# GpSimd's scatters in the scan stage, moved to other slots

## The chip, the cores and the metric

The kernel runs on one core of a Trainium2 chip. The metric is the device time of one execution in microseconds (us): from the program's start to its last output. TensorE (PE) multiplies matrices, VectorE (DVE) and GpSimd (POOL) do elementwise work, ScalarE (ACT) evaluates functions, SyncE (SP) issues most of the data transfers. Each engine runs its own list of instructions in order and waits for the others by semaphores.

## What is computed

The input is 8 sequences of 512 tokens with 256 features. Each goes through a Mamba layer, a residual and a layer norm, and then through a mixture of 8 experts of which each token takes 4, again with residual and norm:

```python
# per sequence, for t in 0..511, with h of 256 x 16:
dA = jnp.exp(dtt[:, :, None] * A)
h = h * dA + dtt[:, :, None] * Bt[:, None, :] * xt[:, :, None]
y = jnp.einsum('bdn,bn->bd', h, Ct) + xt * D
...
x = _layernorm(x + _L0_attn_ref(x, ...))
x = _layernorm(x + _L0_ffn_ref(x, ...))   # router, top 4 of 8 experts, SwiGLU
```

## The kernel before

There are two large stages. In the **scan stage** the 8 sequences run through a pipeline of rounds; in the **expert stage** tiles of 512 rows run through the experts' weights. Between them lies a queue in DRAM for each expert: a token's row (1088 bytes) is copied to the four queues of its experts. These copies are the **scatters** of line 1199: one is an indirect DMA that GpSimd issues, 128 rows long, and a sequence has 16, numbered 0 to 15.

A round has 16 **slots**, one for each of the 16 states of the scan. In round r (0 to 7; rounds 3 to 6 are the passes of a hardware loop of two rounds) the following is done at once:

- Sequence r is scanned. In slot t VectorE multiplies the input by B (`weigh_inputs`, line 1021, from PSUM and SBUF to PSUM) and runs the recurrence over 1024 columns (`scan`, line 1030), with the factors `decay` that ScalarE computes two slots ahead (`decays`, line 811). GpSimd multiplies the state by C (`read_state`, line 1157); in slot t it does this for state t-1. TensorE adds the products up (`sum_states`, line 630), in slot t for state t-2; the last two of a sequence come in slots 0 and 1 of the next round.
- Sequence r+1 is prepared: projection, convolution, SiLU, softplus. VectorE's part are three operations of 1024 columns with both inputs in SBUF: two in slot 11 (lines 994 and 997), one in slot 13 (1004), and in slot 15 `drive` (line 1012), which makes the next sequence's input from two SBUF tensors and goes to PSUM.
- Sequence r-1 is finished: gate in slot 2 (1038), output projection, first norm, residual in slot 9 (line 1046, four operations of 256 columns, both inputs in SBUF), second norm. GpSimd computes 1/sqrt of the variances (`power`, lines 1172 to 1176) in slots 6 and 12, scales by the weights of the norm in slot 7 (`scale`, line 1183) and adds its offset in slot 0 (`add_offset`, line 1190).
- Sequence r-2 is routed: TensorE transposes its rows in slot 0 (line 654) and multiplies by the router (664) in slot 1; VectorE ranks the experts in slot 2 (1054 to 1068), takes TensorE's counts (676) in slot 5 (1087) and makes the list of places in slot 6 (1076 to 1133), after which its scatters 0 to 8 may go out.
- Sequence r-3's scatters 9 to 15 go out in the early slots.

`while_scanning` sets where GpSimd's read stands against VectorE: in every slot the read waits until VectorE's weighing of that slot is through, and in slots 2, 6, 9, 11, 13 and 15 until its other work of the slot is through as well. Scatters stand ahead of these waits, so they can run while VectorE does that work. Which slot issues which scatters is set by two tables, `SCATTERS` and `LATE_SCATTERS`. A read of slot 15 waits for `drive`; TensorE's work is in the order of its list, so its routing in slots 0 and 1 of a round stands behind the sum of state 14 of the round before, that is behind the read of slot 15.

Of the kernel before, what the change touches and what calls it, by code (L numbers as in the profile page):

```python
# [164 lines left out]
def build(nc, ctx, ins, out):  # L165
# [983 lines left out]
    def pool_stage1(pool):  # L1149
# [43 lines left out]
        def scatter(s, some):  # L1193
            if 0 in some:
                pool.wait_ge(s_index, s.n + 1)
                after(pool, s_scrap, s.n)
                pool.tensor_tensor(scrap[:, 1:2], neg_half[:, 0:1], neg_half[:, 0:1], ALU.mult).then_inc(s_scrap, 1)
            for i in some:
                pool.indirect_dma_start(queues, bass.IndirectOffsetOnAxis(ap=index[s.p][:, i:i + 1], axis=0),  # L1199
                                        rows[s.p][:, i // TOPK, :], None).then_inc(s_scat[s.p], 16)  # L1200


        SCATTERS = {8: (0,), 9: (1,), 10: (2,), 11: (3,), 12: (4,), 13: (5,), 14: (6, 7), 15: (8,)}
        LATE_SCATTERS = {0: (9,), 3: (10, 11), 4: (12,), 5: (13,), 6: (14,), 7: (15,)}

        def while_scanning(r, t):

# [22 lines left out]
        for r in rounds(pool):  # L1230
            for t in range(SLOTS):
                if r.d and t in SCATTERS:
                    scatter(r.s.at(-2), SCATTERS[t])
                if r.e and r.b and t in LATE_SCATTERS:
                    scatter(r.s.at(-3), LATE_SCATTERS[t])
                if r.c and t == 5:
# [298 lines left out]
    with nc.Block() as block:  # L1535
        @block.tensor
        def _(pe):
            pe_stage1(pe)
            pe_stage2(pe)

        @block.scalar
        def _(act):
            act_stage1(act)
            act_stage2(act)

        @block.vector
        def _(dve):
            dve_stage2(dve, dve_stage1(dve))

        @block.gpsimd  # L1550
        def _(pool):
            pool_stage1(pool)
            pool_stage2(pool)

        @block.sync
        def _(sp):
            sp_stage1(sp)
            last_p = sp_stage2(sp)
            waits = [(s_w[0], 16 * (last_p + 2)), (s_rows[0], 16 * (last_p + 2))]
            waits += [(s_add[i], ADDS * (last_p + 1)) for i in range(2)]  # L1560
            stage2_ends.extend(waits)
# [113 lines left out]
```

## Time and profile before

| | us |
|---|---|
| median of three runs | 1388.95 |
| lowest and highest | 1387.88 and 1389.89 |
| the profiled execution | 1384.42 |
| its span, first to last instruction | 1382.6 |
| VectorE busy | 1076.9 (78%) |
| TensorE busy | 1184.9 (86%) |
| GpSimd busy | 792.0 (57%) |
| ScalarE busy | 898.3 (65%) |

The scan stage takes roughly the first half: the first weighing starts at 37 us, the last scan ends at 612 us, and the last scatters are out at about 693 us. The expert stage is in full swing from 700 us. Busy shares over the whole span mix the two, so the scan stage has to be read by itself: by timelines of a round, by the busy time of a stretch, and by what each engine waited for.

### The profile page before, as it was taken

How to read it: one execution, taken by the hardware profiler on the slowest of the kernel's cores; microseconds unless marked ns; L12 is line 12 of the kernel's file. 1: busy time of each engine (PE TensorE's matmuls, PEld its weight loads, DVE VectorE, ACT ScalarE, POOL GpSimd, SP SyncE). 2: the span in 40 equal slices, each digit the busy share in tenths (PEclk: the TensorE clock that was granted, in tenths of full speed). 3: DMA queues.
4: the chain of work that ended last, by engine and by line, in shares of the span. 5: the costliest groups of instructions: out<-in, count | busy, mean ns of one | idle time of the engine just before them, and what ended most of it. 6: DMA issues, size and time to landing. Idle time of an engine off the chain costs nothing. (4 is left out here: it accounts for less than half of the span.)

```text
span 1382.6 us, 18067 instructions
## 1 busy us (share of the span) xinstructions
PE 1184.9 (86%) x5138; PEld 807.7 (58%) x5138; DVE 1076.9 (78%) x1558; ACT 898.3 (65%) x1551; POOL 792.0 (57%) x567
## 2 busy tenths in 40 slices
PE   7869697978889797665699999999999999999940
PEld 3324252524334343323588888888888888888840
DVE  3999899999999999993757777777777777777744
ACT  4765859484857667424557677677677776767734
POOL 0557568788888888895734444444344444444442
PEclk9999999999989898996799999999999999999985
DMA  2543435444354445325855555655566555565537
GB/s 104 196 154 126 165 122 175 147 167 166 140 190 154 169 154 186 119 103 211 300 156 146 140 146 155 161 158 158 157 158 160 143 141 143 154 161 158 158 38 244
DMA packets 69258, 217.18 MB, mean 157 GB/s; under 512 B 7520, under 2 KB 43232, under 8 KB 56288
## 3 DMA queue, kind: packets, MB, share of 16 engines
q1 hardware_dynamic: 29664, 167.42, 33.5%
q0 software_dynamic: 26880, 36.72, 15.4%
q10 hardware_dynamic: 12672, 12.58, 2.8%
q8 instruction: 14, 0.23, 0.1%
q14 instruction: 28, 0.23, 0.0%
HBM read 165.54 MB, written 51.15 MB: 157 GB/s over the span
## 5 line engine op out<-in xcount | busy, mean ns | idle before, releaser
L630 PE MATMUL p_y<-read,small 128*128 128x512 f32 x512 | 274.0, 668 | 81.5 <-POOL read L1157 81.2
L1030 DVE TENSOR_TENSOR_SCAN state<-decay,p_bu 128x1024 f32<-128x1024 f32 x128 | 292.4, 2285 | 13.3 <-DVE p_bu L1021 5.5
L1486 POOL DMA_INDIRECT total<-o_v,tok x144 | 267.0, 1854 | 45.7 <-issue 45.7
L630 PEld LDWEIGHTS p_y<-read,small 128*128 128x128 f32 x512 | 100.7, 207 | 234.5 <-POOL read L1157 130.0
L1484 POOL TENSOR_TENSOR scrap<-neg_half 128x1 f32<-128x1 f32 x36 | 12.3, 340 | 325.3 <-ACT o_v L1383 322.6
L811 ACT ACTIVATE decay<-dt,scan_rate 128x511 f32<-128x511 f32 x256 | 164.8, 710 | 22.1 <-DVE state L1030 21.9
L1157 POOL TENSOR_TENSOR read<-state,bc 128x1024 f32<-128x1024 f32 x64 | 150.6, 2353 | 29.4 <-DVE p_bu L1021 10.7
L505 ACT ACTIVATE gate_v<-p_g,bias 128x512 f32<-128x512 f32 x144 | 98.4, 683 | 105.8 <-PE p_up L495 103.3
L1199 POOL DMA_INDIRECT queues<-rows,index x128 | 134.8, 1053 | 28.9 <-issue 26.2
L1370 ACT ACTIVATE ah<-a_v 128x512 fp32r<-128x512 f32 x144 | 91.1, 633 | 90.3 <-DVE a_v L1431 90.3
L1157 POOL TENSOR_TENSOR read<-state,first_wh 128x1024 f32<-128x1024 f32 x32 | 75.4, 2355 | 79.9 <-DVE p_bu L1021 48.5
L1420 DVE TENSOR_SCALAR up_v<-up_v 128x512 f32<-128x512 f32 x144 | 61.4, 426 | 62.5 <-ACT up_v L508 62.5
L1426 DVE TENSOR_TENSOR al<-a_v,ah 128x512 fp32r<-128x512 f32 x144 | 98.7, 685 | 13.4 <-ACT ah L1370 13.4
L1431 DVE SCALAR_TENSOR_TENSOR a_v<-gate_v,up_v 128x512 f32<-128x512 f32 x144 | 99.9, 694 | 4.9
L508 ACT ACTIVATE up_v<-p_up,bias 128x512 f32<-128x512 f32 x144 | 98.0, 681 | 0.0
L1157 POOL TENSOR_TENSOR read<-state,first_wl 128x1024 f32<-128x1024 f32 x32 | 75.3, 2354 | 32.7 <-DVE first_raw L997 16.6
L1021 DVE TENSOR_TENSOR p_bu<-p_u,bc 128x1024 f32<-128x1024 f32 x64 | 78.9, 1233 | 7.0 <-DVE state L1030 0.5
L1343 PE MATMUL p_o<-wh,ah 128*128 128x256 f32 x288 | 81.9, 284 | 1.7 <-DVE al L1426 1.7
L1343 PE MATMUL p_o<-first_wh,ah 128*128 128x256 f32 x288 | 83.2, 289 | 0.0
L1343 PE MATMUL p_o<-first_wl,ah 128*128 128x256 f32 x288 | 81.5, 283 | 0.0
L1343 PE MATMUL p_o<-first_wh,al 128*128 128x256 f32 x288 | 81.4, 283 | 0.0
L1343 PE MATMUL p_o<-wh,al 128*128 128x256 f32 x288 | 80.4, 279 | 0.0
(222 smaller groups left out, 3038.4 us busy)
## 6 DMA issues: line engine op xcount, KB each, us to landing
bc<-bc_rows SPq DMA_DIRECT2D x32, 1024.0 KB, 4.8
first_raw<-in_w_experts SPq DMA_DIRECT2D x19, 1668.0 KB, 6.8
raw_w<-in_w_experts SPq DMA_DIRECT2D x18, 1668.0 KB, 6.8
first_wh<-bc_rows SPq DMA_DIRECT2D x16, 1024.0 KB, 5.0
first_wl<-bc_rows SPq DMA_DIRECT2D x16, 1024.0 KB, 4.8
first_rows<-queues SPq DMA_DIRECT2D x19, 544.0 KB, 6.8
xq<-queues SPq DMA_DIRECT2D x18, 544.0 KB, 6.9
queues<-pad SPq DMA_DIRECT2D x9, 544.0 KB, 4.4
```

The costliest lines, as they stand in the source:

```text
L505: act.activation(gate_v[i % 2][:, :], p_g[i % 2][:, :], ACT.Silu, bias=bias[t.p][:, 0, i:i + 1], scale=ALPHA)
L508: act.activation(up_v[i % 2][:, :], p_up[i % 2][:, :], ACT.Identity, bias=bias[t.p][:, 1, i:i + 1])\
L630: mm = pe.matmul(p_y[h][:, :], ident[:, :], read[:, t % 4, h, :], start=False, stop=(t == SLOTS - 1))
L811: act.activation(decay[t % AHEAD][:, h, 1:LEN], dt[s.p][:, h, 1:LEN], ACT.Exp, scale=rate[:, h, t:t + 1])\
L1030: dve.tensor_tensor_scan(flat(state[t % 4][:, :, :]), flat(decay[t % AHEAD][:, :, :]), p_bu[:, :], 0.0, ALU.mult, ALU.add).then_inc(s_stat ...
L1157: pool.tensor_tensor(read[:, t % 4, :, :], state[t % 4][:, :, :], of_state(t, 1), ALU.mult).then_inc(s_read, 1)
L1199: pool.indirect_dma_start(queues, bass.IndirectOffsetOnAxis(ap=index[s.p][:, i:i + 1], axis=0), rows[s.p][:, i // TOPK, :], None).then_inc ...
L1343: mm = pe.matmul(to, v[:, i, a * P:(a + 1) * P], w[t.p][:, c:c + D], start=(i == 0 and a % 2 == 0 and m == 0), stop=(i == CH - 1 and m == ...
L1370: act.activation(ah[:, i, :], a_v[i % 2][:, :], ACT.Copy).then_inc(s_ah, 1)
L1426: dve.tensor_tensor(al[:, i, :], a_v[i % 2][:, :], ah[:, i, :].bitcast(F32), ALU.subtract).then_inc(s_al, 1)
L1431: dve.scalar_tensor_tensor(a_v[i % 2][:, :], gate_v[i % 2][:, :], TOP, up_v[i % 2][:, :], ALU.min, ALU.mult)\
L1486: pool.indirect_dma_start(total, bass.IndirectOffsetOnAxis(ap=tok[t.p][:, a:a + 1], axis=0), o_v[t.p][:, a, :], None, compute_op=ALU.add). ...
```

## The change

The two tables that say in which slot GpSimd issues which scatters are replaced. Nothing is added or removed: a sequence still has 16 scatters, with the same indices and rows.

```diff
-        SCATTERS = {8: (0,), 9: (1,), 10: (2,), 11: (3,), 12: (4,), 13: (5,), 14: (6, 7), 15: (8,)}
-        LATE_SCATTERS = {0: (9,), 3: (10, 11), 4: (12,), 5: (13,), 6: (14,), 7: (15,)}
+        SCATTERS = {9: (0, 1), 11: (2, 3, 4), 13: (5, 6), 15: (7, 8)}
+        LATE_SCATTERS = {2: (9, 10, 11), 3: (12,), 4: (13,), 6: (14, 15)}
```

**Slots 7 to 9 of a loop round, GpSimd, before.** The first row is the end of `power`; line 1183 is the scaling, 1197 a mark ahead of scatter 0, and 1208 the wait for the weighing ahead of a read.

```order
L1176 TENSOR_TENSOR neg_mean<-neg_mean,rstd 128x4
L1199 DMA queues<-rows,index 37376x272
L1208 REGISTER_ALU
L1157 TENSOR_TENSOR read<-state,bc 128x1024
L1183 TENSOR_TENSOR z<-z,small 128x1024
L1197 TENSOR_TENSOR scrap<-neg_half 128x1
L1199 DMA queues<-rows,index 37376x272
L1208 REGISTER_ALU
L1157 TENSOR_TENSOR read<-state,bc 128x1024
L1199 DMA queues<-rows,index 37376x272
L1208 REGISTER_ALU
L1157 TENSOR_TENSOR read<-state,first_wh 128x1024
```

The same place in the changed kernel:

```order
L1176 TENSOR_TENSOR neg_mean<-neg_mean,rstd 128x4
L1208 REGISTER_ALU
L1157 TENSOR_TENSOR read<-state,bc 128x1024
L1183 TENSOR_TENSOR z<-z,small 128x1024
L1208 REGISTER_ALU
L1157 TENSOR_TENSOR read<-state,bc 128x1024
L1197 TENSOR_TENSOR scrap<-neg_half 128x1
L1199 DMA queues<-rows,index 37376x272 x2
L1208 REGISTER_ALU
L1157 TENSOR_TENSOR read<-state,first_wh 128x1024
```

The scatters of slots 7 and 8 are gone; the read of slot 8 (state 7) now stands ahead of every scatter here, and two scatters stand between it and the read of slot 9.

**Slots 13 to 15 of a loop round, GpSimd, before.** The first row is the end of the second `power`; the three reads are those of slots 13, 14 and 15 (states 12, 13 and 14).

```order
L1176 TENSOR_TENSOR neg_mean<-neg_mean,rstd 128x4
L1199 DMA queues<-rows,index 37376x272
L1208 REGISTER_ALU
L1157 TENSOR_TENSOR read<-state,bc 128x1024
L1199 DMA queues<-rows,index 37376x272 x2
L1208 REGISTER_ALU
L1157 TENSOR_TENSOR read<-state,bc 128x1024
L1199 DMA queues<-rows,index 37376x272
L1208 REGISTER_ALU
L1157 TENSOR_TENSOR read<-state,bc 128x1024
```

And after the change:

```order
L1176 TENSOR_TENSOR neg_mean<-neg_mean,rstd 128x4
L1199 DMA queues<-rows,index 37376x272 x2
L1208 REGISTER_ALU
L1157 TENSOR_TENSOR read<-state,bc 128x1024
L1208 REGISTER_ALU
L1157 TENSOR_TENSOR read<-state,bc 128x1024
L1199 DMA queues<-rows,index 37376x272 x2
L1208 REGISTER_ALU
L1157 TENSOR_TENSOR read<-state,bc 128x1024
```

Four scatters stand here in both. One more is ahead of the first read, two fewer between the first and the second, and one more between the second and the third.

## Rows read from the trace of the kernel before

**Rows 1.** Busy us (instructions) of each engine, granted clock, DMA share, round 5:

```profile
400.00:475.00 75.00, 65.17 (x170) 29.34 (x169) 70.91 (x69) 50.68 (x90) 63.00 (x47) 0.91 0.48 164
```

**Rows 2.** Timeline of slot 9, round 5, GpSimd, then VectorE: start, us, what:

```profile
435.51 2.37 POOL L1157 TENSOR_TENSOR read<-state,bc 128x1024 f32<-128x1024 f32 x1
...
435.84 2.33 DVE L1046 SCALAR_TENSOR_TENSOR z<-z,x 128x256 f32<-128x256 f32 x1
...
438.10 0.41 DVE L1046 SCALAR_TENSOR_TENSOR z<-z,x 128x256 f32<-128x256 f32 x1
```

**Rows 3.** Timeline, slots 13 to 15 of round 5, GpSimd:

```profile
457.54 1.05 POOL L1199 DMA_INDIRECT queues<-rows,index  x1 [0.17 <-DVE dt L1004]
...
462.45 0.97 POOL L1199 DMA_INDIRECT queues<-rows,index  x1 [0.30 <-issue]
463.45 2.35 POOL L1157 TENSOR_TENSOR read<-state,bc 128x1024 f32<-128x1024 f32 x1
465.96 1.80 POOL L1199 DMA_INDIRECT queues<-rows,index  x1 [0.17 <-issue]
467.80 2.35 POOL L1157 TENSOR_TENSOR read<-state,bc 128x1024 f32<-128x1024 f32 x1
```

**Rows 4.** Timeline, slot 15, VectorE: rounds 5 and 0:

```profile
464.70 2.20 DVE L1012 TENSOR_TENSOR p_u<-dt,xc 128x1024 f32<-128x1024 f32 x1
...
96.61 1.23 DVE L1012 TENSOR_TENSOR p_u<-dt,xc 128x1024 f32<-128x1024 f32 x1
```

**Rows 5.** Timeline, slots 7 to 11, rounds 5, 6 and 2; brackets: idle before, and releaser:

```profile
428.43 0.20 POOL L1176 TENSOR_TENSOR neg_mean<-neg_mean,rstd 128x4 f32<-128x4 f32 x1
...
428.67 2.07 ACT L848 ACTIVATE z<-z,neg_mean,rstd 128x256 f32<-128x256 f32 x4 [2.23 <-POOL neg_mean L1176]
...
447.23 2.56 ACT L811 ACTIVATE decay<-dt,scan_rate 128x511 f32<-128x511 f32 x4
...
448.75 2.28 DVE L1030 TENSOR_TENSOR_SCAN state<-decay,p_bu 128x1024 f32<-128x1024 f32 x1
...
516.95 1.23 DVE L1021 TENSOR_TENSOR p_bu<-p_u,first_wl 128x1024 f32<-128x1024 f32 x1 [0.46 <-DVE state L1030]
...
222.18 1.95 ACT L811 ACTIVATE decay<-dt,scan_rate 128x511 f32<-128x511 f32 x3
...
223.60 2.29 DVE L1030 TENSOR_TENSOR_SCAN state<-decay,p_bu 128x1024 f32<-128x1024 f32 x1 [0.93 <-issue]
```

**Rows 6.** Timeline, TensorE from round 5's slot 0 to 5; VectorE's slot 5, rounds 5, 6:

```profile
395.16 3.78 PE L630 MATMUL p_y<-read,small 128*128 128x512 f32 x4 [0.57 <-POOL read L1157]
398.73 1.16 PE L654 MATMUL p_bank<-small,rows 128*128 128x128 f32 x8
...
416.91 1.88 PE L630 MATMUL p_y<-read,small 128*128 128x512 f32 x4
418.63 0.18 PE L672 MATMUL p_bank<-chosen,before 128*128 128x40 bf16 x1
...
418.94 0.19 DVE L1087 TENSOR_TENSOR place<-p_bank,base 128x32 f32<-128x32 f32 x1
...
494.01 0.19 DVE L1087 TENSOR_TENSOR place<-p_bank,base 128x32 f32<-128x32 f32 x1 [0.43 <-PE p_bank L676]
```

**Rows 7.** Busy us of a stretch of round 7 and the tail of it:

```profile
573.80:617.70 43.90, 25.27 (x46) 8.59 (x46) 42.68 (x29) 14.90 (x30) 41.19 (x33) 0.88 0.31 111
```

**Rows 8.** Timeline behind the scans, VectorE and GpSimd; the last row is a group of them:

```profile
645.65 2.36 DVE L469 TENSOR_TENSOR first_wl<-first_raw,first_wh 128x1024 fp32r<-128x1024 f32 x2
...
645.91 1.80 POOL L1199 DMA_INDIRECT queues<-rows,index  x1 [0.30 <-issue]
...
661.62 1.11 POOL L1199 DMA_INDIRECT queues<-rows,index  x1 [0.30 <-issue]
...
661.81 0.42 DVE L1061 TENSOR_TENSOR cmp<-lg 128x256 f32<-128x256 f32 x1
...
L1061 DVE TENSOR_TENSOR cmp<-lg 128x256 f32<-128x256 f32 x8 | 3.3, 418 | 0.0
```

**Rows 9.** TensorE's clock: busy and granted clock of two stretches, and sums in round 4:

```profile
386.00:399.00 13.00, 11.39 (x14) 4.01 (x15) 12.50 (x7) 5.93 (x8) 12.19 (x8) 0.50 0.62 205
...
390.81 3.78 PE L630 MATMUL p_y<-read,small 128*128 128x512 f32 x4 [1.04 <-POOL read L1157]
...
315.61 1.98 PE L630 MATMUL p_y<-read,small 128*128 128x512 f32 x4 [1.44 <-POOL read L1157]
```

## The prediction

> **What bounds the kernel now.** I read the busy time of one round first, then the timelines of VectorE and GpSimd slot by slot, and then, wherever VectorE would come free earlier, the timeline of the engine that it waits for next. In round 5 VectorE is busy 70.9 us of 75, TensorE 65.2, GpSimd 63.0, ScalarE 50.7 [rows 1]. So VectorE looks like the bound, and it looks as if it were held up twice a round by GpSimd. In slot 9 the first of four residual operations takes 2.33 us and the others 0.41; it began at 435.84, and GpSimd's read, which began at 435.51, ended at 437.88, 0.3 us before it [rows 2]. In slot 15 `drive` takes 2.20 us, against 1.23 in round 0, where no read runs beside it; the read of round 5 ended at 465.80 [rows 3, 4]. That is 1.92 and 0.97 us in each round. The weighings and scans have one input in PSUM and keep their times beside any read.
>
> Two other chains run just behind VectorE. **ScalarE's**: GpSimd's `power` ends at 428.63, ScalarE starts the norm at 428.67 after waiting 2.23 us for it, and then has norm, convolution, SiLU, softplus and four table loads to do until it starts the decay of slot 11 at 447.23; half of a pair and its latency later, at 447.23 + 1.28 + 0.14 = 448.65, the scan of slot 11 may start. It started at 448.75 [rows 5]. In round 2 the decay starts at 222.18 and the scan at 223.60, and VectorE had stood idle 0.93 us for it. **TensorE's**: from the sum of state 14 (395.16, after a wait for GpSimd's read) it works without a gap until the counts at 418.63, and VectorE takes these in slot 5 at 418.94, in round 6 after 0.43 us of idling [rows 6]. Both chains begin at GpSimd: one at `power` of slot 6, which stands behind a read that waits for VectorE's list of places, the other at the read of slot 15.
>
> **The change part by part.**
>
> Slots 7 to 9. Two scatters of 1.05 and 1.00 us with their lead (about 0.17 each, and a mark of 0.2) leave the way of the read of slot 8. It starts about 2.5 us earlier, at 433.0, and ends at 435.35; the residual's first operation begins at 435.84. So the residual finds no read beside it: 2.33 - 0.41 = 1.92 us less in slot 9, rounds 2 to 7. Scatters 0 and 1 run beside the residual instead.
>
> Slot 11. What VectorE has won it now waits for: the decay of slot 11 hangs on `power` in slot 6, which the change leaves where it is, since the read ahead of it waits for VectorE's places anyway. Of the 1.92 us only the slack there counts: 0.1 in rounds 3 and 5 (448.75 - 448.65), and 0.46 in rounds 4 and 6, where VectorE lost a further 0.36 between scan and weighing [rows 5]; nothing in round 2. Sum over rounds 2 to 6: **1.1 us**.
>
> Slots 13 to 15. Counting from 457.54, when `power` is through: two scatters (1.05 + 0.30 + 0.97) and two reads of 2.35 end at about 464.5 instead of 465.80 [rows 3]. `drive` starts at 464.6, and is over in 1.23 us: 0.97 less for VectorE. But the read of slot 15 does not come earlier. Scatter 7 is now issued just as `drive` starts, and scatters wait for such an operation: the one at 465.96 took 1.80 us and ended 0.86 after `drive` [rows 3, 4], and behind the scans one took 1.80 us and ended 0.86 after the first of two wide operations [rows 8]. So: `drive` ends at 465.8, scatter 7 at 466.7, scatter 8 after 0.30 + 0.97 at 467.95, the read starts at 467.97; before it was 467.80. TensorE's chain to the counts therefore starts at the same time to within 0.2 us, and VectorE, 1 us early, waits for them in slot 5. The 0.97 us count once only, in the pass from round 6 to 7, since round 7 prepares no further sequence and TensorE's counts come early there: **1.2 us**, with the 0.2 that VectorE waits in a middling round.
>
> Slots 2, 3, 4 and 6 take the late scatters. In slot 2 GpSimd otherwise waits some 4.2 us for the ranking, and three scatters take 3 x 1.27 = 3.8 us of it; in slot 6 it waits for the places and two scatters fit. The cover is thin by 0.4 us in slot 2, and what exceeds it delays the read of slot 2, for which nobody waits until TensorE's sum behind the output projection. Cost 0. VectorE's small operations do not feel a scatter: 0.42 us with one beside it, 0.418 as the mean of the eight rounds [rows 8].
>
> Round 7. From the list of places to the last read GpSimd is busy 41.2 us of 43.9, the rest being mostly lead times [rows 7]: there it is the bound, since VectorE has no second sequence to prepare. The change takes scatter 15 (1.05 + 0.17) out of this stretch into the wait of slot 6: **1.2 us**. VectorE gets its 1.92 us and more in slot 9 and the reads do not follow.
>
> This far 1.1 + 1.2 + 1.2 = 3.5 us, less about 0.3 for the 0.17 us by which the read of slot 15 is later in some rounds: **3.2 us**.
>
> **TensorE's clock.** In the last slots of a round TensorE has stood idle 4.2 us and then runs the sums of states 12, 13 and 14 at 1.2 GHz: granted clock 0.50 from 386 to 399, 3.78 us a sum; in round 3's last slots one took 1.98 us, at 2.4 GHz [rows 9]. The sum of state 14 at the head of the chain to the counts costs 3.78 us at the low clock and 1.88 at the full one [rows 6]. After the change sums 12 and 13 run without the 1.04 us between them (the first read is 1.3 us later, the second 1.3 earlier), behind a longer idle time of some 5.3 us. If the clock is back before sum 14, the counts come 1.9 us earlier, of which VectorE can use 0.97 + 0.1 to 0.5 = about 1.5. At most four rounds (3 to 6) can gain: 0 to 6 us. The trace has both outcomes, three rounds low to one partly full, and the denser pair of sums makes the full one likelier; I take one and a half of four rounds, **2.3 us**.
>
> One rule speaks against this change. The Trainium skill ("SBUF — State Buffer", section "Who interferes with whom") says that a VectorE instruction with two SBUF inputs and a GpSimd instruction that reads SBUF exclude each other for the whole instruction, and that the one issued first keeps the other out. For reads beside the residual and `drive` this trace agrees (2.33 against 0.41 us, 2.20 against 1.23). Taken literally for scatters, which read their indices, it would let each hold up VectorE for its 1.0 us; rival 1 works that out from rows.
>
> **The rivals.**
>
> 1. *Scatters hold VectorE* (slower). If a scatter that starts first keeps a following two-input operation waiting, three in slot 2 and two in slot 6 do so. Slot 6 is on the path to `power` and ScalarE's chain: up to 1 us in each of six rounds; of slot 2's 3 us, 1 to 2 remain after the slack in slot 5. Some 2 us x 5 rounds = 10 us, less 3.2: about 1396. It decides from 0.6 us a round. Against it: no small operation in the trace is longer beside a scatter, and the second of two wide operations kept its pace while a scatter slipped between them (2.36 us for two) [rows 8].
> 2. *The read of slot 15 comes later, or the clock back later.* If scatter 8 too is stretched, or the longer idle time keeps the low clock over one more sum (1.9 us), the counts come 0.5 to 1 us later in each of five rounds: 2.5 to 5 us against 3.2. Time 1386.5 to 1391, about no change.
> 3. *The read of slot 8 still overlaps the residual.* The margin is 0.5 us in the loop, none in round 7. Then slot 9 changes nothing; because of slot 11 this costs only the 1.1 us: 1386.9. No change.
> 4. *VectorE is the bound after all.* If ScalarE's and TensorE's chains give way, (1.92 + 0.97) x 5 rounds + 1.2 = 15.7 us: 1373. Against it: the idle 0.93 us in round 2 and 0.43 in round 6 [rows 5, 6].
>
> **How the numbers follow.** The profiled execution is 1384.42 us (span 1382.6), 4.5 below the median of 1388.95; the sum is a difference and is taken off the median. Forecast: 1388.95 - 3.2 - 2.3 = **1383.5**; its own range is 1380 (clock back in every round) to 1386.5 (in none, and a loss in the handover of 0.8). Chances: forecast 0.62, rival 1 0.08, rival 2 0.18, rival 3 0.07, rival 4 0.05. The range for 8 in 10 takes in rivals 2 and 3 for the most part: 1379.5 to 1388.5. A measurement of this kernel tells about 0.2% (2.8 us) from nothing. The forecast without the clock lies just past that line, so of its 0.62 some 0.10 count as the same: faster 0.57, same 0.34, slower 0.09.
>
> **What the profile after would show.** Step by step: the first residual operation near 0.41 us in rounds 2 to 7; `drive` near 1.23; the scan of slot 11 now idle before it, waiting for the decay, 1.8 us in the loop; the read of slot 15 ending as long after the scan of slot 11 as before, 21.4 us; VectorE idle for the counts by over 1 us in slot 5, unless the sum of state 14 takes 1.9 us; rounds 3 to 6 of 75.1 us only 0 to 1.7 us shorter; no VectorE operation longer beside a scatter. Wrong would be: rounds shorter by the whole 2.9 us (rival 4), small operations of slots 2 and 6 stretched (rival 1), or GpSimd's stretch of round 7 unchanged.

## The result, and the profile after

| | before | after |
|---|---|---|
| median, us | 1388.41 (6 runs) | 1382.48 (6 runs) |
| lowest and highest | 1386.46 and 1392.66 | 1379.58 and 1384.90 |
| the profiled execution | 1384.42 | 1382.49 |
| its span | 1382.6 | 1380.5 |

The ratio of after to before is 0.9954, with a 95% interval from 0.9937 to 0.9970: the change gains 0.3 to 0.6%. The forecast was 1383.5 us, with a range from 1379.5 to 1388.5.

Where VectorE's time went is told by its groups of instructions over the loop's four rounds and a slot (columns: line, engine, operation, tiles, count | busy us, mean ns | idle us before them, by what ended most of it). Before, from 243 to 550 us:

```profile
L1030 DVE TENSOR_TENSOR_SCAN state<-decay,p_bu 128x1024 f32<-128x1024 f32 x67 | 153.0, 2284 | 8.9 <-DVE p_bu L1021 5.5 <-POOL read L1157 1.6 <-ACT decay L811 0.8
...
L1046 DVE SCALAR_TENSOR_TENSOR z<-z,x 128x256 f32<-128x256 f32 x16 | 13.4, 891 | 0.0
L1012 DVE TENSOR_TENSOR p_u<-dt,xc 128x1024 f32<-128x1024 f32 x4 | 8.8, 2190 | 0.1
```

After, the same stretch:

```profile
L1030 DVE TENSOR_TENSOR_SCAN state<-decay,p_bu 128x1024 f32<-128x1024 f32 x67 | 153.1, 2285 | 14.3 <-ACT decay L811 7.3 <-DVE p_bu L1021 5.4 <-issue 0.8
...
L1021 DVE TENSOR_TENSOR p_bu<-p_u,first_wh 128x1024 f32<-128x1024 f32 x18 | 22.2, 1233 | 4.8 <-issue 3.1
...
L1046 DVE SCALAR_TENSOR_TENSOR z<-z,x 128x256 f32<-128x256 f32 x16 | 5.9, 426 | 0.0
L1012 DVE TENSOR_TENSOR p_u<-dt,xc 128x1024 f32<-128x1024 f32 x4 | 5.0, 1256 | 0.1
```

The residual is 7.5 us shorter in four rounds and `drive` 3.8 us. Against it stand 6.5 us of waiting for ScalarE's `decay`, and 3.1 us of idle time before a weighing that nothing in the profile ends ("issue"). No term of the forecast had the last one.

By rounds, with the start of each round's first weighing (the last row is the end of the last read):

| round | start before | start after | length before | length after | difference |
|---|---|---|---|---|---|
| 2 | 170.10 | 171.16 | 73.72 | 72.69 | -1.03 |
| 3 | 243.82 | 243.85 | 75.13 | 73.89 | -1.24 |
| 4 | 318.95 | 317.74 | 75.13 | 76.51 | +1.38, of it 3.11 a pause |
| 5 | 394.08 | 394.25 | 75.11 | 74.07 | -1.04 |
| 6 | 469.19 | 468.32 | 75.45 | 73.54 | -1.91 |
| 7 | 544.64 | 541.86 | 73.05 | 72.08 | -0.97 |
| end | 617.69 | 613.94 | | | |

Rounds 2 to 7 gain 7.9 us, the pause takes 3.1 back, and 1.06 us were lost before round 2 in this execution: 3.75 us less at the last read. The expert stage's part of the span is 764.9 us before and 766.6 after, with the same code; over all kernels below it lies between 760 and 769. So one profiled execution does not tell a few us of the total, and the medians have to.

Part of that difference has a place. Behind the scans VectorE takes the counts of the last sequence (line 1087). Before, then after with TensorE's end of the same counts ahead of it:

```profile
666.14 0.19 DVE L1087 TENSOR_TENSOR place<-p_bank,base 128x32 f32<-128x32 f32 x1 [1.79 <-PE p_bank L676]
...
661.24 0.24 PE L676 MATMUL p_bank<-chosen,ones 128*128 128x32 bf16 x4
665.02 0.19 DVE L1087 TENSOR_TENSOR place<-p_bank,base 128x32 f32<-128x32 f32 x1 [5.75 <-remote]
```

Before, VectorE takes them 0.04 us behind TensorE; in the changed kernel 3.54 us behind it, so that of the 3.75 us only 1.1 are left when the last list of places is ready (668.36 and 667.23). Of the fourteen traces of this document, five have such a wait, of 3.5 to 3.9 us (after, x_early, slot15_x_early, decay_first_2, decay_first_2x); in the other nine it is 0.04 us. What ends it the profile does not say ("remote"), and its cause is open.

**Slot 9 of round 5**, GpSimd, then VectorE, as in [rows 2]:

```profile
433.08 2.35 POOL L1157 TENSOR_TENSOR read<-state,bc 128x1024 f32<-128x1024 f32 x1
...
435.73 1.04 POOL L1199 DMA_INDIRECT queues<-rows,index  x1 [0.15 <-issue]
...
436.05 0.42 DVE L1046 SCALAR_TENSOR_TENSOR z<-z,x 128x256 f32<-128x256 f32 x1
```

The read of slot 8 ends at 435.43, 0.6 us ahead of the residual, and a scatter runs beside it; the operation takes 0.42 us.

**Slot 11 of round 5**, VectorE and ScalarE, as in [rows 5]:

```profile
428.64 0.20 POOL L1176 TENSOR_TENSOR neg_mean<-neg_mean,rstd 128x4 f32<-128x4 f32 x1
...
447.44 2.56 ACT L811 ACTIVATE decay<-dt,scan_rate 128x511 f32<-128x511 f32 x4
...
448.80 2.29 DVE L1030 TENSOR_TENSOR_SCAN state<-decay,p_bu 128x1024 f32<-128x1024 f32 x1 [1.42 <-ACT decay L811]
```

From the end of `power` to the scan it is 20.0 us (448.80 - 428.84), before it was 20.1 (448.75 - 428.63): ScalarE's chain is as long as it was, and VectorE now stands still 1.42 us for it.

**Slots 13 to 15 of round 5**, GpSimd, then `drive`, as in [rows 3, 4]:

```profile
457.60 1.04 POOL L1199 DMA_INDIRECT queues<-rows,index  x1 [0.16 <-DVE dt L1004]
...
459.94 4.66 POOL L1157 TENSOR_TENSOR read<-state,bc 128x1024 f32<-128x1024 f32 x2
464.76 1.00 POOL L1199 DMA_INDIRECT queues<-rows,index  x1 [0.17 <-issue]
466.06 0.96 POOL L1199 DMA_INDIRECT queues<-rows,index  x1 [0.30 <-issue]
467.04 2.36 POOL L1157 TENSOR_TENSOR read<-state,bc 128x1024 f32<-128x1024 f32 x1
...
464.76 1.26 DVE L1012 TENSOR_TENSOR p_u<-dt,xc 128x1024 f32<-128x1024 f32 x1
```

Scatter 7 and `drive` start at the same instant and neither is longer for it, so the read of slot 15 starts at 467.04, not at 467.97 as forecast.

**TensorE's chain to the counts**, end of round 5 and round 6, as in [rows 6, 9]; the last row is VectorE's:

```profile
462.35 5.77 PE L630 MATMUL p_y<-read,small 128*128 128x512 f32 x8 [5.46 <-POOL read L1157]
469.45 1.98 PE L630 MATMUL p_y<-read,small 128*128 128x512 f32 x4 [1.34 <-POOL read L1157]
...
492.36 0.18 PE L672 MATMUL p_bank<-chosen,before 128*128 128x40 bf16 x1
...
492.67 0.19 DVE L1087 TENSOR_TENSOR place<-p_bank,base 128x32 f32<-128x32 f32 x1
```

The sum of state 14 takes 1.98 us, TensorE's upper clock of 2.4 GHz, and VectorE takes the counts without a wait; before it was 3.78 and a wait of 0.43.

**The pause**, VectorE at the end of round 4 and the start of round 5:

```profile
387.70 1.25 DVE L1012 TENSOR_TENSOR p_u<-dt,xc 128x1024 f32<-128x1024 f32 x1
388.87 2.27 DVE L1030 TENSOR_TENSOR_SCAN state<-decay,p_bu 128x1024 f32<-128x1024 f32 x1
394.25 1.23 DVE L1021 TENSOR_TENSOR p_bu<-p_u,first_wh 128x1024 f32<-128x1024 f32 x1 [3.11 <-issue]
```

Between rounds 4 and 5 the hardware loop jumps back, the only time that it does. In the kernel before the scan of slot 15 started at 391.77, and the weighing followed without a gap at 394.08.

### The profile page after: what moved, and what is told of

Same layout as the page of the kernel before. It is cut to its first block and busy times, and to the rows that moved or that the text cites. A ratio compares the mean times of both kernels' runs of the same rounds, so it can differ in the third digit from the quotient of the medians.

```text
span 1380.5 us, 18065 instructions
## 1 busy us (share of the span) xinstructions
PE 1178.1 (85%) x5138; PEld 806.3 (58%) x5138; DVE 1062.1 (77%) x1558; ACT 898.4 (65%) x1551; POOL 792.2 (57%) x567
## 5 line engine op out<-in xcount | busy, mean ns | idle before, releaser
L630 PE MATMUL p_y<-read,small 128*128 128x512 f32 x512 | 266.7, 657 | 81.7 <-POOL read L1157 81.7
```

Source lines behind the costliest of these rows:

```text
L630: mm = pe.matmul(p_y[h][:, :], ident[:, :], read[:, t % 4, h, :], start=False, stop=(t == SLOTS - 1))
```

## The experiments

They come in three groups: the two halves of the change, ScalarE's chain, and the pause. The kernel before was measured anew beside each set of them, with medians of 1385.28, 1388.23 and 1383.97 us. So kernels of different sets are compared by their ratios to it and not by their times.

### The two halves apart

**Slots 8 and 9 alone (slot9).**

```diff
-        SCATTERS = {8: (0,), 9: (1,), 10: (2,), 11: (3,), 12: (4,), 13: (5,), 14: (6, 7), 15: (8,)}
-        LATE_SCATTERS = {0: (9,), 3: (10, 11), 4: (12,), 5: (13,), 6: (14,), 7: (15,)}
+        SCATTERS = {9: (0, 1), 10: (2,), 11: (3,), 12: (4,), 13: (5,), 14: (6, 7), 15: (8,)}
+        LATE_SCATTERS = {0: (9,), 3: (10, 11), 4: (12,), 5: (13,), 6: (14, 15)}
```

> The kernel before with the slot 7 to 9 part of the change alone: scatter 15 of a sequence goes out in slot 6 instead of 7, scatter 0 in slot 9 instead of 8; all other scatters where they were. Theory A (ScalarE's chain takes the gain of slot 9 back in slot 11): the first residual operation falls from 2.33 to about 0.42 us, the scan of slot 11 then idles for its decay, and a loop round is only 0.1 to 0.5 us shorter than 75.1; round 7 about 1 to 2 us shorter. Total 2 to 3 us faster, ratio 0.998 to 0.9985. Theory B (VectorE is the bound): 1.9 us a round, six rounds, 11.5 us faster, ratio 0.992.

Measured: 1382.20 us against 1385.28, ratio 0.9975 [0.9964, 0.9987]. VectorE in slots 9 and 11 of round 5:

```profile
437.11 0.41 DVE L1046 SCALAR_TENSOR_TENSOR z<-z,x 128x256 f32<-128x256 f32 x1
...
450.08 2.29 DVE L1030 TENSOR_TENSOR_SCAN state<-decay,p_bu 128x1024 f32<-128x1024 f32 x1 [1.42 <-ACT decay L811]
```

The residual has its 1.92 us, and the rounds 3 to 6 take 75.04, 74.86, 75.04 and 74.76 us instead of 75.13, 75.13, 75.11 and 75.45: the gain is given back two slots later, as the prediction has it. Rounds 2 to 7 together are 1.7 us shorter in this trace; the medians differ by 3.1.

**Slots 13 to 15 alone (slot15).**

```diff
-        SCATTERS = {8: (0,), 9: (1,), 10: (2,), 11: (3,), 12: (4,), 13: (5,), 14: (6, 7), 15: (8,)}
+        SCATTERS = {8: (0,), 9: (1,), 10: (2,), 11: (3,), 12: (4,), 13: (5, 6), 15: (7, 8)}
```

> The kernel before with the slot 13 to 15 part alone: scatters 5 and 6 in slot 13, none in slot 14, 7 and 8 in slot 15. Theory A (this part carries the gain of the loop rounds, through the earlier read of slot 15 and TensorE's full clock): drive 1.25 instead of 2.20 us, the read of slot 15 ends about 0.8 us sooner after the scan of slot 11 than before (20.6 instead of 21.4), the sum of state 14 takes 1.98 us, and a loop round is 0.9 to 1.2 us shorter: 5 to 6 us faster in all, ratio 0.996. Theory B (the parts only work together): under 2 us, ratio 0.999.

Measured: 1385.80 against 1385.28, ratio 1.0011 [0.9996, 1.0026]: nothing. The trace shows `drive` at 1.26 us and the read of slot 15 0.8 us earlier, and two places where it was lost: the pause, and once the counts.

```profile
397.10 1.23 DVE L1021 TENSOR_TENSOR p_bu<-p_u,first_wh 128x1024 f32<-128x1024 f32 x1 [3.30 <-issue]
...
425.31 0.19 DVE L1087 TENSOR_TENSOR place<-p_bank,base 128x32 f32<-128x32 f32 x1 [3.43 <-PE p_bank L676]
```

TensorE was idle during the pause too, and ran the routing slowly, as at the lower clock:

```profile
400.98 2.77 PE L630 MATMUL p_y<-read,small 128*128 128x512 f32 x4 [3.07 <-POOL read L1157]
403.54 3.42 PE L664 MATMUL p_bank<-small,x1t 128*128 128x8 f32 x16
```

Line 664 takes 1.85 us for 16 in slot15_x_early and slot15_bc_late (below), which have the same tables and the same pause, and no late counts in round 5. So the pause alone does not make the second wait; the two together cost this execution 6.7 us. Without them its rounds 2 to 7 are 4.9 us shorter than before, and the median shows no gain in any of the three kernels with these tables.

By the ratios the halves alone give 3.5 us and -1.5 us, the whole change 6.4. What each half brings to the whole is therefore shown for the rounds of single traces, and not for the time.

**Scatter 6 in slot 15 too (six15)**, meant to make the read of slot 15 late.

```diff
-        SCATTERS = {9: (0, 1), 11: (2, 3, 4), 13: (5, 6), 15: (7, 8)}
+        SCATTERS = {9: (0, 1), 11: (2, 3, 4), 13: (5,), 15: (6, 7, 8)}
```

> The changed kernel with scatter 6 taken from slot 13 to slot 15, so that three scatters (6, 7, 8) stand ahead of the read of slot 15: that read comes 1.27 us later. Theory A (TensorE's chain from this read to the counts stands close behind VectorE, with some 0.3 us to spare in the changed kernel): VectorE idles about 1 us for the counts in slot 5 of rounds 3 to 7, and the kernel is 4 to 5 us slower than the changed one, 1387 us. Theory B (VectorE alone sets the round): no idling there, and within 1 us of the changed kernel, 1382.5.

Measured: 1381.15 against 1385.28, ratio 0.9971 [0.9956, 0.9986], about as the change. It did not do what it was for: without scatter 6 in slot 13 GpSimd came to slot 15 1.3 us earlier, and the third scatter took just this time, so that the read ended as early as in the changed kernel, 20.6 us behind the start of the scan of slot 11. It tells nothing on TensorE's chain. The pause was there (3.39 us).

### ScalarE's chain

**The decay of slot 11 ahead of the softplus (decay_first)**, on top of the change. VectorE's two operations behind the softplus and GpSimd's scatters of slot 11 go to slot 12.

```diff
+                if r.a and r.b and t == 9:
+                    decays(r.s, 11)
                 if r.a and t == 9:
                     softplus(r)
...
-                if r.b and t < SLOTS - AHEAD + 2:
+                if r.b and t < SLOTS - AHEAD + 2 and not (r.a and t == 9):
                     decays(r.s, t + AHEAD - 2)
...
-                if r.a and t == (11 if r.b else 10):
+                if r.a and t == (12 if r.b else 10):
...
-        SCATTERS = {9: (0, 1), 11: (2, 3, 4), 13: (5, 6), 15: (7, 8)}
+        SCATTERS = {9: (0, 1), 12: (2, 3, 4), 13: (5, 6), 15: (7, 8)}
...
-            if r.a and t == 11:
+            if r.a and t == 12:
```

> The changed kernel with the decay of slot 11 computed ahead of the softplus in ScalarE's slot 9 instead of behind it, VectorE's two softplus operations in slot 12 instead of 11, and scatters 2 to 4 with them in slot 12. Theory A (the scan of slot 11 waits for ScalarE's chain, 1.4 us a round): slot 11 takes 3.8 us, slot 12 5.8, the wait for the decay is gone, and rounds 2 to 6 are 1.3 to 1.7 us shorter: 7 us faster than the changed kernel, 1375.5. Theory B (the wait only moves: softplus ends 1.3 us later and VectorE waits for it in slot 12, or for TensorE's counts in slot 5): within 1.5 us of the changed kernel.

Measured: 1366.77 against 1385.28, ratio 0.9869 [0.9842, 0.9897], the fastest of all. VectorE's groups from 239.6 to 540 us (lines are two further down than before):

```profile
L1032 DVE TENSOR_TENSOR_SCAN state<-decay,p_bu 128x1024 f32<-128x1024 f32 x66 | 150.8, 2285 | 8.9 <-DVE p_bu L1023 7.3 <-ACT decay L811 0.8
...
L1014 DVE TENSOR_TENSOR p_u<-dt,xc 128x1024 f32<-128x1024 f32 x4 | 8.2, 2044 | 0.1
L1048 DVE SCALAR_TENSOR_TENSOR z<-z,x 128x256 f32<-128x256 f32 x16 | 6.0, 429 | 0.0
```

The wait for `decay` is back at 0.8 us for all rounds, the residual keeps its gain, and rounds 3 to 5 take 72.97, 72.86 and 72.96 us (round 6 74.48, with 1.23 us of waiting for the counts). `drive` has a read beside it again (2.04 us), and there is no pause.

**The same with the old tables (decay_first_old)**: the kernel before with ScalarE's, VectorE's and the wait's edit, and no scatter moved.

> The kernel before, scatter tables as they are, with the decay of slot 11 alone ahead of the softplus, and VectorE's two operations behind the softplus in slot 12. Theory A, ScalarE's chain holds VectorE only once its slot 9 is shorter: in the kernel before its slack is 0.1 us in two rounds and VectorE stood idle 0.93 us in round 2 and never in the loop, so the edit alone gives at most 1 to 3 us (ratio 0.998 to 1.000), and the 13 us that it gave on top of the change come from the two together (1.92 us a round in slot 9 that now count). Theory B, ScalarE's chain costs VectorE time in the kernel before as well, by the order of the work in slots 9 to 12 and not by the wait: the edit alone gives 5 us or more (0.996 or below).

Measured: 1380.43 against 1383.97, ratio 0.9976 [0.9965, 0.9987], some 3.3 us. In the loop the rounds gain 0.16, 0.24, 0.14 and 0.47 us. So the early decay gives little where slot 9 is long, and the short slot 9 gives little where the decay is late. Both together: rounds 3 to 5 of decay_first are 2.00, 2.03 and 2.01 us shorter than those of decay_first_old, which is slot 9's 1.92 us, now in full. Two chains that end almost at the same time have to be shortened both.

In time, the change alone gives some 6.4 us (0.9954 of 1385), the early decay alone 3.3, and both 18.1, with an interval from 14.3 to 21.9. Not all of this is accounted for: at the last read decay_first is 11.7 us ahead of the kernel before (606.01 against 617.69), the change 3.8 and decay_first_old 2.8. Of the 5.2 us that the two edits give beyond their sum there, 3.1 are the pause, which decay_first does not have.

**The short `drive` on top (decay_first_2)**: scatter 2 in slot 11 and 3 and 4 in slot 12, so that the reads come earlier.

```diff
-        SCATTERS = {9: (0, 1), 12: (2, 3, 4), 13: (5, 6), 15: (7, 8)}
+        SCATTERS = {9: (0, 1), 11: (2,), 12: (3, 4), 13: (5, 6), 15: (7, 8)}
```

> The kernel with the early decay of slot 11, and scatter 2 in slot 11, 3 and 4 in slot 12, instead of all three in slot 12. In the former, GpSimd came 1.3 us too late through slots 12 to 14, so that its read ran beside drive, which took 2.04 us. Theory: drive takes 1.25 us again and the rounds are 0.8 us shorter, 72.1 instead of 72.9: 4 us faster than that kernel, ratio 0.984; but if the gap at the loop's jump comes back with the earlier scatters of slot 15, 3 us of it are lost, ratio 0.986 to 0.987.

Measured: 1373.46 against 1388.23, ratio 0.9892 [0.9874, 0.9911]. `drive` takes 1.27 us and rounds 5 and 6 only 72.37 and 72.22, but the pause is back with 3.20 us. It was not faster than decay_first; the two intervals overlap. The last read ends at 604.50, against 606.01 there, but from then to the end it is 767.4 us, against 762.1, with the same code: this trace has the late counts of the last sequence (3.5 us) and that of decay_first has not.

### The pause

The six kernels here ask what VectorE waits for at the jump. Every kernel of the series whose `drive` takes 1.25 to 1.29 us in round 4 has the pause, and those whose `drive` takes 2.04 or more have not.

**The load of x two slots earlier (x_early, slot15_x_early, decay_first_2x)**: ScalarE's queue loads 512 KB in slot 14, just ahead of the jump. The edit is the same on the changed kernel, on slot15 and on decay_first_2:

```diff
-                if r.b and t == 14:
+                if r.b and t == 12:
```

> The changed kernel with ScalarE's load of x (512 KB) issued in slot 12 instead of slot 14, so that it no longer runs with the write to total and the replication of B and C at the end of a round. In the profiles of every kernel with the slot 15 part of the change VectorE stands idle 3.1 to 3.4 us, with no releaser, ahead of slot 0 of round 5, which is where the hardware loop jumps back, while the DMA engines are busy all the time. Theory A (its next instructions are fetched behind that traffic): the gap falls below 1 us, and the kernel is 3 us faster than the changed one, 0.994 of the kernel before or less. Theory B (the gap belongs to the jump and has nothing to do with the traffic): it stays at 3 us and the time stays that of the changed kernel, ratio 0.996.

> The kernel before with the slot 13 to 15 part alone, which gained nothing (ratio 1.001), and the load of x in slot 12. Theory A (that part does win 0.9 to 1.4 us in each loop round, and gave it back in the gap at the loop's jump and in the counts of round 5, which came 3.4 us late behind it): no gap, no late counts, rounds 3 to 6 of 73.9 to 74.3 us, 4 to 6 us faster than before, ratio 0.996 to 0.997. Theory B: ratio 0.999 to 1.001 again.

> The same as the former, with the load of x in slot 12 as well. Theory: as the former without a gap at the loop's jump, ratio 0.984 or a little less. If the former has no gap either, the two are equal.

Measured: ratios 0.9955 [0.9939, 0.9970], 1.0006 [0.9997, 1.0015] and 0.9894 [0.9880, 0.9909], each as without the edit. The pauses are 3.25, 3.08 and 3.52 us: the load of x is not the cause.

**The replication of B and C one read later (bc_late, slot15_bc_late, decay_first_2_bc_late)**: SyncE copies 1 MB, rows of B and C replicated over the partitions, as soon as the read of slot 14 is through.

```diff
-            after(sp, s_read, SLOTS * s.n + 2 * (pair - RING + 1))
+            after(sp, s_read, SLOTS * s.n + 2 * (pair - RING + 1) + 1)
```

> The changed kernel, with SyncE's replication of B and C (1 MB, line 1284) waiting for one more read of GpSimd: at the end of a round it goes out behind the read of state 14 instead of state 13, some 2.3 us later. Nothing else moves. Theory A, the pause of 3.1 us that VectorE makes between the last scan of round 4 and the first weighing of round 5 is its wait for its own instructions, fetched by DMA at the jump back of the hardware loop, and these stand behind the replication, which in the changed kernel goes out 1.3 us or more ahead of the scan of slot 15 (before: 0.99 us): the pause is below 0.5 us, round 4 takes about 73.5 us instead of 76.5, and the time is 3 us below the changed kernel's, a ratio of about 0.993 to the kernel before. Theory B, the replication has nothing to do with it (the jump waits for something else that the shorter `drive` uncovers): the pause stays at 3.0 to 3.5 us and the ratio at 0.9954. Theory C, the later replication is late for the scan that needs it: VectorE waits for DMA in the middle of a round, and the time is above the changed kernel's.

> The kernel before with the slots 13 to 15 of the change alone (scatters 5 and 6 in slot 13, 7 and 8 in slot 15), and the replication one read later. The slot-15 part alone measured 1.0011 [0.9996, 1.0026], with a pause of 3.3 us at the loop's jump. Theory A, the part is worth its 0.97 us a round and the pause ate it: without the pause the ratio is 0.996 to 0.998. Theory B, TensorE's counts hold VectorE anyway, as the prediction has it: the pause is gone, but VectorE waits 0.5 to 1 us for the counts in slot 5 of the loop's rounds, rounds of 75.1 us stay at 74.5 or more, and the ratio is 0.998 to 1.000.

> The changed kernel with the decay of slot 11 ahead of the softplus (which VectorE and GpSimd take in slot 12), scatters 0 and 1 in slot 9, 2 in 11, 3 and 4 in 12, 5 and 6 in 13, 7 and 8 in 15, and the replication one read later. The same kernel without the last measured 0.9892 with a pause of 3.2 us, and decay_first, without pause but with a `drive` of 2.04 us, 0.9869. Theory A, the replication makes the pause: it is gone, rounds 3 to 6 take 72.2 to 73.4 us, and the ratio is 0.985 to 0.987, the lowest so far. Theory B, not the replication: the ratio stays at 0.989.

Measured: ratios 0.9969 [0.9957, 0.9980], 1.0009 [0.9993, 1.0024] and 0.9921 [0.9898, 0.9944]; pauses of 3.41, 3.16 and 3.20 us. The expectation of theory A failed in all three. The expectation of bc_late also has a mistake: it says that nothing else moves. In the trace of bc_late the replication before this one (`first_wl`) and the load of x_t behind it on SyncE's queue moved as well, from 378 to 385.5, and so into the stretch ahead of the jump. SyncE's queue there:

```profile
385.46 0.32 SPq L1286 DMA_DIRECT2D first_wl<-bc_rows  x1
385.82 1.29 SPq L1269 DMA_DIRECT2D first_raw<-in_x_t  x1
392.56 0.32 SPq L1286 DMA_DIRECT2D bc<-bc_rows  x1
```

So one transfer of 1 MB was taken away and another put in its place, and the edit could not tell the theories apart.

**What the transfers show.** The view of DMA traffic counts, for a stretch, the packets of each queue (queue, kind: packets, MB, share of 16 engines). q14 brings instructions, q1 what SyncE issues. In the kernel before, from 391.3 to 391.6, and then from 391.6 to 394:

```profile
q14 instruction: 1, 0.01, 7.4%
...
q1 hardware_dynamic: 94, 0.77, 101.7%
```

The fetch comes just ahead of the replication, on engines that are otherwise nearly idle, 0.4 us before the scan of slot 15 starts; then the replication has all the engines. In the changed kernel, from 388.7 to 392, and from 392 to 392.3:

```profile
q1 hardware_dynamic: 127, 0.97, 92.1%
q0 software_dynamic: 12, 0.05, 3.8%
...
q0 software_dynamic: 36, 0.12, 96.2%
q14 instruction: 1, 0.01, 6.4%
q1 hardware_dynamic: 7, 0.00, 1.3%
```

Here no instruction comes for 3.3 us, while the replication is on its way, and one as its last packets go; 2 us later VectorE weighs. In bc_late, from 388.7 to 391.9, it is the transfer of `first_wl` that is on its way, and the fetches come behind it, from 392 to 392.6:

```profile
q1 hardware_dynamic: 146, 1.05, 96.9%
...
q14 instruction: 2, 0.02, 6.4%
```

Set beside each other, with the start of `drive` in round 4 and the issue of the 1 MB transfer that is on the way behind it:

| kernel | `drive` starts | transfer issued | pause |
|---|---|---|---|
| before | 389.66 | 390.78 | none |
| slot9 | 391.08 | 392.18 | none |
| decay_first_old | 387.16 | 388.29 | none |
| decay_first | 381.14 | 382.11 | none |
| after | 387.70 | 387.55 | 3.11 |
| slot15 | 390.34 | 390.20 | 3.30 |
| six15 | 389.81 | 388.41 | 3.39 |
| x_early | 387.83 | 387.67 | 3.25 |
| slot15_x_early | 392.06 | 391.91 | 3.08 |
| decay_first_2 | 381.16 | 381.03 | 3.20 |
| decay_first_2x | 380.76 | 380.63 | 3.52 |
| bc_late | 387.89 | 385.46 | 3.41 |
| slot15_bc_late | 388.94 | 386.50 | 3.16 |
| decay_first_2_bc_late | 380.29 | 377.85 | 3.20 |

The order of the two separates all fourteen, as the length of `drive` does. It also tells why a short `drive` and the pause come together. SyncE issues the replication when the read of slot 14 ends. `drive` is short only if that read has ended before it starts, and then the transfer is out before VectorE gets to the jump. The time of the instruction packet says more. Looked for in steps of 0.05 us, it stands 2.2 to 2.3 us ahead of the weighing in all ten kernels with a pause. In before, slot9 and decay_first_old it stands 2.7 to 2.8 us ahead of it, and in decay_first 2.27 us, as in the ten. So the weighing of slot 0 seems to need some 2.2 us from this packet on, and the pause is as long as the packet is late.

What makes the packet late is a reading: VectorE's fetch of its instructions at the jump waits behind a 1 MB transfer that was queued first. The Trainium skill ("Runtime: NRT & Kernel Launch", section "Instruction fetch mechanics") says that a taken branch to code which the sequencer does not hold forces a fetch by DMA before the engine can go on; this trace agrees as far as its instruction packet goes, and the page does not say what such a fetch waits for. Three things don't fit so easily. In x_early the DMA engines carry nothing at all from 386.9 to 388.8, and no instruction is fetched then either, so the request came later than that or waits for more than free engines. (In the four traces without a pause the packet comes 1.65 to 2.0 us behind the start of `drive`; in x_early that would be 389.5, when the transfer is on its way.)

```profile
DMA packets 0, 0.00 MB, mean 0 GB/s; under 512 B 0, under 2 KB 0, under 8 KB 0
```

In six15 the transfer's queue moves three packets from 393.6 to 394.2 and none after, GpSimd's scatters have the engines, and the instruction packet comes only at 394.5. And the trace of slot15_bc_late has rounds 2 to 7 5.3 us shorter without the pause, 2.1 with it, while its median says +1.2 us with an interval from -1.0 to +3.3; what the other executions of the slot-15 kernels lose beyond the pause stays open. A second reading is not ruled out: in all ten the packet comes 0.9 to 1.3 us behind the end of the scan of slot 15, however early the transfer was issued (2.4 us ahead of `drive` in bc_late, 0.15 in the changed kernel). So VectorE might ask for it only there, and earlier where `drive` is long. The fetch's owner among the engines is not in the records, and no kernel was run in which no large transfer was on its way at the jump with a short `drive`. So the cause is argued from fourteen traces and not shown by taking it away.

## Why the prediction was right, and where it was not

The time came out within 1.0 us of the forecast. That is in good part luck: the steps added up to 5.5 us, the rounds gained 7.9, and the pause, which no step had, took 3.1 back. The late counts behind the scans, which no step had either, took 3.5 in the profiled execution.

- **Slot 9: right.** 0.41 to 0.42 us for the first residual operation, and no read beside it in any of rounds 2 to 7, round 7 included, where no margin was seen.
- **Slot 11: right.** The 1.92 us wait for `decay`. The prediction had 0.1 us left in rounds 3 and 5 and 0.46 in 4 and 6, and slot9's rounds gain 0.09, 0.27, 0.07 and 0.69 (0.24 of the last is a shorter wait for the counts). The idle time ahead of the scan is 1.42 us in rounds 3 and 5 and 1.3 in 4 and 6, not 1.8; the rest is lost earlier in the slot, most of it between lines 994 and 997 (0.20 us in round 5; 0.38 in slot9's trace, waiting for ScalarE's `x1t`).
- **`drive`: right in size (1.25 us), wrong in its worth.** The step that failed is "the read of slot 15 does not come earlier". I had scatter 7 held for the whole of `drive`, from one that started 1.26 us after it [rows 3, 4]. In rounds 3 to 6 it started at the same instant and took 1.00 us; so the read ends 20.6 us behind the scan of slot 11, not 21.4. Only in round 2, where it started 0.07 us after `drive`, was it stretched, and to the forecast size:

```profile
240.46 2.03 POOL L1199 DMA_INDIRECT queues<-rows,index  x1 [0.17 <-issue]
...
240.39 1.23 DVE L1012 TENSOR_TENSOR p_u<-dt,xc 128x1024 f32<-128x1024 f32 x1
```

- **The counts: wrong.** With the read earlier and the clock back, VectorE waits for them 0.1 us at most in rounds 3 to 6. So the 0.97 us count in every round and not once: rounds 3 and 5 gain 1.24 and 1.04, rounds 4 and 6, with the 0.46 of slot 11 and the waits of 0.2 and 0.4 for the counts gone, 1.7 (without the pause) and 1.91.
- **TensorE's clock: right in direction, undersized.** The sum of state 14 takes 1.98 us in all of the four rounds, not in one and a half. In x_early and bc_late it is so in three of four, and the fourth waits 1.16 and 1.17 us for the counts; the term varies with the execution.
- **Round 7: right.** From the start of the read of slot 6 to the end of the last read 42.5 us instead of 43.8, for a forecast of 1.2 us less. GpSimd there:

```profile
571.43 2.33 POOL L1157 TENSOR_TENSOR read<-state,bc 128x1024 f32<-128x1024 f32 x1 [1.09 <-issue]
...
609.29 4.65 POOL L1157 TENSOR_TENSOR read<-state,bc 128x1024 f32<-128x1024 f32 x2
```

- **Slots 2, 3, 4 and 6: right.** The last of slot 2's three scatters ends at 406.13, and the read then still waits for VectorE. Line 1061 takes 419 ns as the mean of eight rounds, 418 before: rival 1 is off.

```profile
405.06 1.07 POOL L1199 DMA_INDIRECT queues<-rows,index  x1 [0.30 <-issue]
407.91 2.36 POOL L1157 TENSOR_TENSOR read<-state,first_wh 128x1024 f32<-128x1024 f32 x1 [1.77 <-DVE ex L1068]
...
L1061 DVE TENSOR_TENSOR cmp<-lg 128x256 f32<-128x256 f32 x8 | 3.3, 419 | 0.0
```

- **The jump of the loop: missing.** The prediction asked, for each wait removed, what is late next, and took the next engine for the answer. It did not ask what the earlier end of a read sets off: SyncE's transfer, which goes out 1.3 us earlier against the scan of slot 15.

Rival 4, VectorE the bound after all, was off while ScalarE's chain stood. It named 1373 us, a ratio of 0.9885 to the 1388.95 of before; decay_first, which moves the decay out of the way, reached 0.9869, with a `drive` that was still long.

Two prices of the rivals are not what the prediction's own terms give. Rival 3's 1386.9 takes 1.1 us off the 3.2 and leaves the clock's 2.3 out without saying so; with them it is 1384.6. Rival 2's 2.5 to 5 us against 3.2 give 1388.3 to 1390.8, not 1386.5 to 1391. Neither came.

## What to carry to other kernels

Before a gain in one slot is counted, follow it to the next wait on the same engine: here 1.9 us a round were paid back two slots later by an engine whose slack was 0.1 us, and together with an edit of that engine's order, worth 3.3 us by itself, the change gave some 18 us instead of 6. When a change makes an operation end earlier, list the transfers that its end releases, and look at what they then run ahead of; a loop's jump back is such a place. Two steps of a forecast that fail in opposite directions look like a good forecast, so check each against its own row.

## What the runs showed of the hardware

- **A pause of 3.1 to 3.5 us at the jump back of a hardware loop**, where a 1 MB transfer was issued before the engine's last wide operation, and none where it was issued 0.97 us or more behind that operation's start (fourteen traces). In the ten with a pause the weighing started 2.2 to 2.3 us behind an instruction packet of 8 KB. That the transfer makes the packet late is not shown.
- **A scatter waits for a VectorE operation with two SBUF inputs that was first, and does not hold up one that comes after it.** Scatter first or at the same instant: 1.00 us, and `drive` keeps its 1.25. Scatter 0.07 us later: 2.03 us, ending 0.87 us after `drive`. The Trainium skill ("SBUF — State Buffer", section "Who interferes with whom") has the one issued first keep the other out, in both directions. For a scatter behind a wide operation the trace agrees; a scatter that was first did not hold VectorE in any row here (0.42 us for the residual with one beside it).
